# Router and feature maps of a fused four-layer kernel's first stage: expert mask by match-and-replace, relu as a ScalarE pass, residual added by an identity matmul

## The reference

```
# layer 1: linear attention, feature map elu + 1
q, k, v = split(x @ W, 3);  q = elu(q) + 1;  k = elu(k) + 1
KV = einsum('bld,blh->bhd', k, v)
Z = 1 / (einsum('bld,bd->bl', q, k.sum(1)) + 1e-6)
x = layernorm(x + einsum('bld,bhd,bl->blh', q, KV, Z))
# layer 2: router, top 4 of 32, and shared expert
probs = softmax(x @ gate_w.T)
topk_w, topk_idx = top_k(probs, 4);  topk_w /= topk_w.sum(-1)
...
shared = (silu(g) * u) @ shared_w_down     # g, u = split(x @ shared_w_gate_up)
x = layernorm(x + routed + shared)
```

## Time and profile before

| | us |
|---|---|
| median of three runs | 2514.21 |
| profiled execution, span | 2515.7 |
| VectorE busy | 2154.8 (86%) |
| TensorE matmul busy | 1786.1 (71%) |
| GpSimd busy | 1118.2 (44%) |
| ScalarE busy | 1035.9 (41%) |

### The profile page before, as it was taken

The page is one execution under the profiler, slowest core; times in us unless marked ns, Lnnn a source line. Parts: engine busy times, 40 slices in busy tenths (PEclk is TensorE's granted clock), DMA queues, the critical chain, the costliest instruction groups (busy, mean ns, idle before and its releaser), DMA issues.

```text
span 2515.7 us, 24789 instructions
## 1 busy us (share of the span) xinstructions
PE 1786.1 (71%) x6433; PEld 982.1 (39%) x6433; DVE 2154.8 (86%) x3132; ACT 1035.9 (41%) x1722; POOL 1118.2 (44%) x602
## 2 busy tenths in 40 slices
PE   4776104346787887877787878787878787878687
PEld 3454003312344444444344434443444444444344
DVE  4888791139899998999999999999999999999996
ACT  1322000135463545454545444454545354636343
POOL 1101306724556454554455545555454445454540
PEclk7999555567898889898898888898888889989899
DMA  6333102300000000000000000000000000000000
GB/s 168 100 106 98 27 1 39 37 17 8 5 5 9 5 9 5 8 4 9 5 9 4 9 5 9 4 13 1 13 0 13 1 13 0 13 1 5 5 1 9
DMA packets 72565, 49.75 MB, mean 20 GB/s; under 512 B 5296, under 2 KB 68432, under 8 KB 72144
## 3 DMA queue, kind: packets, MB, share of 16 engines
q1 hardware_dynamic: 57872, 39.85, 5.5%
q0 software_dynamic: 14592, 8.92, 2.8%
HBM read 27.50 MB, written 21.18 MB: 19 GB/s over the span
## 4 chain that ended last, share of the span: by engine, by line
DVE 35%; PE 26%; issue 22%; POOL 11%; ACT 2%; DMA 1%; SPq 1%; DVEq 1%; POOLq 0%; ACTq 0%
DVE hst L1330 8%; PE bank L906 7%; DVE prod L1343 5%; POOL dbx L528 5%; PE bank L915 3%; PE bank L917 3%; DVE prod L1348 3%; DVE hg L1253 3%; PE bank L934 2%; DVE hh L1266 2%; PE bank L949 1%; DVE cand L1154 1%; DVE val L1157 1%; POOL rwp L506 1%; PE bank L862 1%
## 5 line engine op out<-in xcount | busy, mean ns | idle before, releaser
L528 POOL TENSOR_TENSOR dbx<-u,bs 128x1024 f32<-128x1024 f32 x256 | 719.0, 2818 | 363.9 <-ACT bs L670 232.1
L1330 DVE TENSOR_TENSOR_SCAN hst<-dA,dbx 128x1024 f32<-128x1024 f32 x256 | 675.7, 2639 | 26.2 <-issue 14.6
L906 PE MATMUL bank<-prod,ident 128*128 128x512 f32 x832 | 490.3, 720 | 79.3 <-DVE prod L1348 58.0
L678 ACT ACTIVATE dA<-dt,aneg 128x511 f32<-128x511 f32 x512 | 338.2, 709 | 17.3 <-DVE hst L1330 15.2
L1343 DVE TENSOR_TENSOR prod<-hst,bank 128x1024 f32<-128x1024 f32 x256 | 310.4, 1213 | 19.4 <-PE bank L894 11.2
L670 ACT ACTIVATE bs<-bank 128x512 f32<-128x512 f32 x256 | 151.3, 591 | 338.2 <-PE bank L890 335.4
L906 PEld LDWEIGHTS bank<-prod,ident 128*128 128x128 f32 x832 | 183.3, 226 | 258.3 <-issue 154.7
L691 ACT ACTIVATE ht<-hg 128x512 f32<-128x512 f32 (+1 forms) x208 | 130.8, 629 | 309.5 <-DVE hg L1253 308.3
L915 PE MATMUL bank<-x3T,w_w 128*128 128x512 f32 (+1 forms) x416 | 230.1, 636 | 0.7 <-ACT x3T L696 0.7
L894 PE MATMUL bank<-parts,sel_bc 99*128 99x512 bf16 x256 | 107.6, 420 | 166.0 <-DVE prod L1343 164.2
L917 PE MATMUL bank<-x3T,w_w 128*128 128x512 f32 (+1 forms) x416 | 213.9, 596 | 0.1
(11 more groups left out here) (202 smaller groups left out, 2529.6 us busy)
## 6 DMA issues: line engine op xcount, KB each, us to landing
xg_rows<-xg SPq DMA_DIRECT2D x16, 320.0 KB, 2.5
xt<-in_x SPq DMA_DIRECT2D x16, 256.0 KB, 3.1
xT<-in_xT SPq DMA_DIRECT2D x16, 256.0 KB, 3.4
resid_rows<-zero SPq DMA_DIRECT2D x16, 256.0 KB, 3.4
resid_rows<-resid SPq DMA_DIRECT2D x16, 256.0 KB, 2.4
rin<-resid_rows SPq DMA_DIRECT2D x16, 256.0 KB, 2.8
rin<-resid_rows POOLq DMA_DIRECT2D x16, 256.0 KB, 4.8
out_dram<-ofin SPq DMA_DIRECT2D x16, 256.0 KB, 2.4
```

Of the source, the lines that this page charges most:

```text
L528: gp.tensor_tensor(dbx[n % 2][:, :, :], u[s.par][:, :, :], bs[n % 2][:, :].rearrange("p (h t) -> p h t", h=1).to_broadcast([P, NH, SEQ]), ...
L678: act.activation(dA[n % 2][:, h, 1:SEQ], dt_[s.par][:, h, 1:SEQ], ACT.Exp, scale=aneg[:, h, n:n + 1]).then_inc(da_rdy, 1)
L906: last = mm(y_ps[:, h, :], ident[:, :], prod[n % 2][:, h, :], start=(sums_to(n) == 1), stop=(n == NS - 1), skip_group_check=True)
L1330: dve.tensor_tensor_scan(flat(hst[n % 2]), flat(dA[n % 2]), flat(dbx[n % 2]), 0.0, ALU.mult, ALU.add).then_inc(scan_rdy, 1)
```

## The change

It does three things in the first stage:
1. The mask of the four chosen experts. Instead of the indices of the largest logits and a comparison with 0..31, the entries 5 to 8 of top are overwritten with a very low constant, the logits that match top are replaced by that constant (rep), and mask is 1 where rep differs from the logits. The replacements stand behind sg, where hot stood.
2. The feature maps. ScalarE makes rk = relu(k) and rq = relu(q) after each exp; VectorE makes kf and qf in one pass each, min(exp, 1) + relu.
3. The residual. TensorE first adds x1 into the shared expert's bank by an identity matmul, behind the wait for hsh; ScalarE copies the sum to resid, ahead of maskT; VectorE's addition goes.

```diff
@@ ScalarE, stage1
-                    act.activation(ek[:, :, :], kv_ps[:, :, 0:D], ACT.Exp).then_inc(ek_rdy, 1)
+                    act.activation(ek[:, :, :], kv_ps[:, :, 0:D], ACT.Exp)
+                    act.activation(rk[:, :, :], kv_ps[:, :, 0:D], ACT.Relu).then_inc(ek_rdy, 1)
...
-                    act.activation(eq[:, :], q_ps[:, :], ACT.Exp).then_inc(eq_rdy, 1)
+                    act.activation(eq[:, :], q_ps[:, :], ACT.Exp)
+                    act.activation(rq[:, :], q_ps[:, :], ACT.Relu).then_inc(eq_rdy, 1)
...
+                    act.wait_ge(d_mm, r.at(1, 1))
+                    need(act, st_r, r.at(16))
+                    act.activation(resid[:, :, :], blk4(d_ps), ACT.Copy).then_inc(resid_rdy, 1)
                     act.wait_ge(mt_mm, r.at(1, 1))
@@ TensorE, stage1
-                    need(pe, rq_rdy, a.at(1))
...
                     pe.wait_ge(hsh_rdy, r.at(1, 1))
                     need(pe, resid_rdy, r.at(1))
-                    for k in range(TT):
-                        last = mm(d_ps[:, tile(k)], hsh[:, tile(k)], wt["sd"][:, :], start=True, stop=True)
+                    mm(d_ps[:, :], ident[:, :], xg[r.par][:, :, 0:D], start=True, stop=False, skip_group_check=True)
+                    for k in range(TT):
+                        last = mm(d_ps[:, tile(k)], hsh[:, tile(k)], wt["sd"][:, :], start=False, stop=True,
+                                  skip_group_check=True)
@@ VectorE, stage1
-                    dve.wait_ge(v_rdy, a.at(1, 1))
-                    ts(rk[:, :, :], kv_ps[:, :, 0:D], 0.0, 1.0, ALU.max, ALU.add).then_inc(rk_rdy, 1)
+                    dve.wait_ge(ek_rdy, a.at(1, 1))
+                    need(dve, kva_mm, a.at(1))
+                    stt(kf[:, :, :], ek[:, :, :], 1.0, rk[:, :, :], ALU.min, ALU.add).then_inc(kf_rdy, 1)
                     dve.wait_ge(eq_rdy, a.at(1, 1))
-                    ts(rq[:, :], q_ps[:, :], 0.0, 1.0, ALU.max, ALU.add).then_inc(rq_rdy, 1)
-                    dve.wait_ge(rk_rdy, a.at(1, 1))
-                    need(dve, kva_mm, a.at(1))
-                    tt(kf[:, :, :], ek[:, :, :], rk[:, :, :], ALU.min).then_inc(kf_rdy, 1)
-                    dve.wait_ge(rq_rdy, a.at(1, 1))
                     need(dve, o_mm, a.at(1))
-                    tt(qf[:, :], eq[:, :], rq[:, :], ALU.min).then_inc(qf_rdy, 1)
+                    stt(qf[:, :], eq[:, :], 1.0, rq[:, :], ALU.min, ALU.add).then_inc(qf_rdy, 1)
...
-                    for k in range(TT):
-                        dve.max_index(topi[:, k, :], top[:, k, :], lg[:, k, :]).then_inc(route0, 1)
+                    dve.memset(top[:, :, TOPK:8], TAKEN).then_inc(route0, 1)
                     dve.wait_ge(tg_rdy, r.at(1, 1))
                     stt(sg[:, :], tg[:, :], 1.0, g_ps[0:I0, :], ALU.add, ALU.mult).then_inc(sg_rdy, 1)
-                    dve.wait_ge(route0, r.at(15, 9))
-                    one_hot(hot, topi, TOPK, E0).then_inc(route0, 1)
+                    dve.wait_ge(route0, r.at(15, 6))
+                    settle(dve)
+                    for k in range(TT):
+                        dve.match_replace(rep[:, k, :], top[:, k, :], lg[:, k, :], TAKEN).then_inc(route0, 1)
...
-                    dve.tensor_reduce(mask[:, :, :], hot[:, :, :, :].rearrange("p t k e -> p t e k"), AX.X, ALU.add
-                                      ).then_inc(route0, 1)
+                    tt(mask[:, :, :], rep[:, :, :], lg[:, :, :], ALU.not_equal).then_inc(route0, 1)
...
-                    dve.wait_ge(d_mm, r.at(1, 1))
-                    need(dve, st_r, r.at(16))
-                    tt(resid[:, :, :], blk4(d_ps), xg[r.par][:, :, 0:D], ALU.add).then_inc(resid_rdy, 1)
```

More of the change, by code:

```diff
@@ L39 @@
 LN_EPS = 1e-5
+TAKEN = -3.0e38
 Z_EPS = 1e-6
@@ L156, in build @@
             top = eb("top", [P, TT, 8])
-            topi = eb("topi", [P, TT, 8], U32)
+            rep = eb("rep", [P, TT, E0])
             lsub = eb("lsub", [P, TT, E0])
             lexp = eb("lexp", [P, TT, E0])
-            hot = eb("hot", [P, TT, TOPK, E0])
             mask = eb("mask", [P, TT, E0])
@@ L261, in build @@
         ldx0, ldx1, kv_mm, q_mm, ek_rdy = sem("ldx0"), sem("ldx1"), sem("kv_mm"), sem("q_mm"), sem("ek_rdy")
-        v_rdy, rk_rdy, kf_rdy, eq_rdy, rq_rdy = sem("v_rdy"), sem("rk_rdy"), sem("kf_rdy"), sem("eq_rdy"), sem("rq_rdy")
+        v_rdy, kf_rdy, eq_rdy = sem("v_rdy"), sem("kf_rdy"), sem("eq_rdy")
         qf_rdy = sem("qf_rdy")
```

## The result

The changed kernel takes 2532.1 us (median, 2528.0 to 2536.1 over four runs) against 2514.2: ratio 1.007, 95% interval 1.005 to 1.0091. A fourth run of the kernel before, 2596.9 us, was a slow one and is left out. The changed kernel is slower, by 18 us in the medians, where 4 us faster was forecast; the profiled execution has a span of 2527.2, 11.5 more than that of before.

What follows compares the result with a forecast made beforehand. A ring of waits through all engines was taken to bound the first stage at 13.63 us per iteration; at 13.35, a gain of 0.28 over 15 iterations, 4.2 us, gave 2510.0 from 2514.2, range 2501 to 2518.

Steps and rivals of the forecast that it cites:

- Third arc: VectorE's stretch from sg to the end of pre, forecast to shrink from 4.44 to 3.73 us, a gain of 0.71.
- pairs at 0.16: Four match-and-replace pairs on VectorE between sg and hsh, priced at 0.16 us each, 0.64 in all.
- Rival B: VectorE's match pairs don't overlap, 0.26 us each: iteration 13.75, kernel 2516.0 us; chance 12%.
- D: Rival on VectorE: den waits for the o matmuls, not for mask; left at 0.10 us of slack, no chance given.
- TensorE's tail: TensorE's end of iteration: the identity matmul, priced 0.91 us, makes L754 start at P + 0.84 instead of P + 0.05.
- ScalarE's queue: Two added Relu passes ahead of x1T on ScalarE, about 0.50 us each, make x1T late by 0.43 us.
- the new ring: Chain sg, hsh, identity matmul, L795, L754, five ScalarE passes, x1T, sg, forecast to set the first-stage iteration at 13.35 us.
- Rival A: Identity matmul or Relu costs less, x1T isn't late, the whole 0.71 us per iteration comes through: 2503.5 us; chance 16%.
- P: The end of pre on VectorE in each first-stage iteration, the point from which the prediction counts times.
- rival C: Relu makes ScalarE load another function table, 1283 ns a load: 2587 us, or 2529 with one per iteration; chance 3%.
- The end of the stage at nothing: Last block's later mask costs nothing, since val waits for GpSimd's third selection with 1.9 us slack; at most +1.6.
- Block 0's gain lost at the xT load: Anything block 0 gains ends at the second L754's wait for its xT load at 37.25, so worth nothing.

Runs made afterwards that it cites:

- e1: Only part 1 (mask by match-and-replace) against the kernel before: 2532.2 us, ratio 1.0062.
- e4: Parts 1 and 3, the changed kernel with the two relu passes left on VectorE, against the kernel before: 2516.3 us, ratio 0.9997.
- e8: The kernel before plus one unread 128x160 VectorE multiplication ahead of hsh, against the kernel before: 2522.0 us, ratio 1.0025.
- e13: The kernel before plus dummy matmuls in TensorE's two front-half waits, nothing of the change, against the kernel before: 2517.2 us, ratio 1.0022.
- e6: The changed kernel plus dummy matmuls, one before the x1 transposes and two before the router logits, against the kernel before: 2512.8 us, ratio 1.0006.
- e3: Only part 3 (identity matmul and ScalarE's resid) against the kernel before: 2519.1 us, ratio 1.0011.
- e5: The changed kernel plus two unread 128x160 VectorE multiplications ahead of hsh, against the kernel before: 2519.0 us, ratio 1.0015.
- e9: Part 1 alone plus three unread 128x170 VectorE multiplications ahead of hsh, against the kernel before: 2514.5 us, ratio 1.0002.
- e7: Part 1 alone plus dummy matmuls, one before the x1 transposes and two before the router logits, against the kernel before: 2504.9 us, ratio 0.9964.
- e14: e7 measured again, on the same chip as e13, against the kernel before: 2503.2 us, ratio 0.9953.
- e12: Part 1 alone plus one dummy matmul before the x1 transposes and one before the logits, against the kernel before: 2508.4 us, ratio 0.9975.

## Why the prediction was wrong

- **Third arc, 3.73 us and pairs at 0.16.** Right. sg at 133.02 to hsh at 134.27 is 1.25 (1.24 forecast); a pair is 146.98 - 146.82 = 0.16; e1's and e4's full-clock iteration is 12.92, as forecast for that arc alone. Rival B fell, and D with it: den at 135.07 has no wait before it.
- **TensorE's tail and ScalarE's queue as the new ring, 13.35 us.** The mechanism is right, the size 0.16 off. From the rows above: hsh to identity 0.73 (0.73), identity 1.05 (0.91), L795 1.09 (1.08), L801 to L759 0.45 (0.61), L759 to ek 1.92 (2.03), five ScalarE passes 2.41 (2.50), x1T to sg 4.29 (4.25), with 1.25 from sg to hsh 13.19. Four terms are off by more than 0.05: the identity matmul costs 0.14 more, above its upper bound of 1.02, while L801 to L759 costs 0.16 less, L759 to ek 0.11 less and the five ScalarE passes 0.09 less. Rival A fell: x1T does come late, by 0.27 us (13.19 - 12.92). A slip without effect: with the Relus left on VectorE, x1T would be ready at P + 0.84 + 2.03 + 1.50 = P + 4.37 by the prediction's own terms, not P + 4.41.
- **Relu without a table load (rival C).** Right to doubt it. ScalarE's loads after are those of before, 33 in all and one of them in the first stage, at its start; the group that answers to the earlier trace rows:

```profile
L670 ACT ACT_TABLE_LOAD x16 | 20.5, 1283 | 0.3
```

- **The end of the stage at nothing.** The two competitors were named, but the load won:

```profile
268.46 12.13 POOL L448 TENSOR_SCALAR_AFFINE_SELECT sel_bc<-sel_bc 99x4224 bf16<-99x4224 bf16 x3
...
271.17 0.59 ACT L603 ACTIVATE maskT<-bank 32x512 f32<-32x512 f32 x1 [0.37 <-PE bank L801]
...
281.03 2.29 DVE L1161 TENSOR_TENSOR val<-val,rev 128x2048 f32<-128x2048 f32 x1 [13.61 <-DMA val<-mask_by_expert]
```

GpSimd ends at 280.59, val starts at 281.03 and takes 2.29 at once, where the earlier trace rows has 4.03. So it was GpSimd's work that held val up before, and val now starts after GpSimd has ended, the sign that the prediction gave for a mispriced end. From the end of pre to the end of val it is 283.32 - 248.73 = 34.6 us against 276.82 - 242.84 = 34.0: 0.6 us lost, within the bound of 1.6.
- **Block 0's gain lost at the xT load.** Not refuted. The second block's k and v matmuls start at 35.11 instead of the 37.25 of the earlier trace rows, 2.1 us earlier. But in e8 and e13, which have nothing of the change, they start at 34.56 and 34.03, and in the sixteen profiled executions anywhere from 31.84 to 37.25, the kernel before being the latest. So these 2 us are a spread between executions, and nothing shows that the change saves them.

The step that failed is none of the sum but what it took for granted in its first part: "the TensorE clock granted is 1.00". The earlier trace rows has that for one iteration, and in the profiled execution it held for all fourteen; the sum then used prices at 2.4 GHz for a kernel that would have another length and another pattern. The lower level was priced once, for the end of the stage, and none of the rivals had it in the iterations. In the first stage the account is: iterations -14 x 0.44 = -6.2, earlier start -2.0 (x1T at 41.41 against 43.38, the spread named above), falls +14.7, together +6.5; measured +6.6 fourteen iterations later (x1T at 240.80 against 234.24). That the falls are the cause is shown from both sides. Taken away by dummies (e6), the fourteen distances take 13.5 us less than in the changed kernel, and the ratio goes from 1.007 to 1.0006. Brought in by part 1 alone, which shortens the iteration and leaves TensorE's work as it is (e1), they make the fourteen distances 22.4 us longer than before (213.24 against 190.86) and the kernel as slow as the changed one. It is no matter of the profiled executions alone: the mean granted clock is listed for every run, and it is 0.833 to 0.836 in the four of the changed kernel and 0.828 to 0.835 in the eight of e1, against 0.840 to 0.848 in 108 of the kernel before.

The Trainium skill, page "TensorE: Matmul & The Clock Gate", section "HAM oscillation — how this bites in real kernels", describes a kernel that pays the transition back to full clock again in every tile because its waits come round in each. By that rule the trace agrees in the repetition: e1 pays it in thirteen of fourteen. It differs in the size of the waits, 3 to 5 us in the page's kernel and 1.35 at most before a fall here. The rule would also name the kernel before as a candidate, with the same waits and not one fall in its profiled execution, and there the trace differs again.

**What stays open.** First, which moment within the light stretch decides. No row tells why e3's iterations of 13.63 us fall five times and then not at all; that the place in time matters is inferred from e3, e5, e8 and e9 and not measured by itself. Second, the last stage: its instructions are the same in all the kernels, and in the sixteen profiled executions it takes 2008.3 to 2017.6 us, at a mean clock of 0.87 to 0.88 where it was read; from the third block on a block takes 119 to 125 us, before and after. Of the 18 us in the medians the first stages account for some 6.5 in the profiled execution, the last stage for 5.0, and the rest was in no profiled execution. Whether the change makes the last stage longer (2017.6, and 2017.2 in e6, 2016.2 in e5, but also 2015.9 in e9 that has only part 1) or whether this is chance can't be settled with one profile of each. The one kernel that has two, e7 and e14, took 2010.0 and 2009.7. Third, the counts of falls are of single executions: whether the kernel before has some in others isn't known, and 108 of its runs spread from 2499.6 to 2524.2 us.

## What to carry to other kernels

Before pricing a shorter iteration, look at the granted clock over many iterations, and at where TensorE has little to do in each: if there is such a stretch, a kernel that never shows a fall may only have a lucky length, and any edit, even one that only removes work, can lose more by the clock than it gains on its path. Put the clock among the rivals with its own price, here 1.6 us or 3 us for a fall with no slack behind it and 0.2 us for one with a wait behind it. Then try the shortened kernel with cheap dummy matmuls in the waits; e7 turned a loss of 0.6% into a gain of 0.4 to 0.5% that way.

## What the runs showed of the hardware

- A fall of the clock costs an iteration of e1 1.6 us (14.56 against 12.92) or 3.2 us (16.1). In the changed kernel the second matmul of the shared expert takes 1.91 at the lower level, against 1.02 before. In e8 a fall whose delay ran into a wait of 1.35 cost 0.17 us.
- Work put into TensorE's waits keeps the clock up at an unchanged length: 13 falls against 2 at 12.92 us (e1, e12), 4 against 0 at 13.87 and 13.88 (e8, e13), in one profiled execution each.
- Adding 0.7 us of VectorE work to every iteration made a kernel 15 to 18 us faster (e1 to e9), and the fastest kernel of all (e7) has 1.4 us more of TensorE work per iteration than the kernel before (11.77 us busy against 10.37).
- e1, which only lightens the first stage, had the most falls; with part 3, which adds the identity matmul to TensorE, there were 5 instead of 13 at the same 12.92 us (e1 to e4).
- A match-and-replace pair on 128x32 takes 0.16 us, as a pair of value load and index search does.
